# Attention and mixture-of-experts kernel on one core: the additions of the output and the second conditionings at other units, and a new order around the last unit

## What is computed

```python
ek = exp(min(f, 30)); ekv = ek * f
a, b = scan forward and backward over tokens: a = a*decay + ekv, b = b*decay + ek
out = sigmoid(r) * (num / max(den, 1e-8)) * (0.8 + 0.2*tf)        # r is x or the later x
x = x + attention(cond(x, f, f))      # 16 heads of 128, causal mask, softmax, output weights W_O
x = x + ffn(cond2(x, f, f))           # 8 experts; top 2 by the logits, softmax of the two as gates
```

## Time and profile before

| | before |
|---|---|
| median of three runs | 371.82 us |
| the profiled execution, its own time | 371.82 us |
| its span (first to last instruction) | 369.9 us |
| busy: TensorE matmul, VectorE, ScalarE, GpSimd | 93%, 86%, 69%, 57% |
| mean granted TensorE clock | 0.995 |

### The profile page before, as it was taken

The page is one execution under the profiler, slowest core; times in us unless marked ns, Lnnn a source line. Parts: engine busy times, 40 slices in busy tenths (PEclk is TensorE's granted clock), DMA queues, the critical chain, the costliest instruction groups (busy, mean ns, idle before and its releaser), DMA issues.

```text
span 369.9 us, 7426 instructions
## 1 busy us (share of the span) xinstructions
PE 344.7 (93%) x2404; PEld 319.4 (86%) x2404; DVE 318.7 (86%) x892; ACT 255.9 (69%) x687; POOL 212.6 (57%) x223
## 2 busy tenths in 40 slices
PE   0796599999999999999999999999999989899997
PEld 0685499998999999989999999999999979788885
DVE  4979899999898989899989999999768576869675
ACT  5669888788878869886888888878778565321100
POOL 1875686855756468867867886787673424210000
PEclk9999989999999999999999999999999999999999
DMA  5670130100000000130100022100000000000000
GB/s 166 240 276 4 57 113 2 59 4 1 2 0 3 1 2 0 52 123 0 28 31 3 1 73 101 58 3 1 2 2 1 2 1 2 0 16 15 28 28 30
DMA packets 4613, 14.13 MB, mean 38 GB/s; under 512 B 848, under 2 KB 1888, under 8 KB 3936
## 3 DMA queue, kind: packets, MB, share of 16 engines
q1 hardware_dynamic: 4352, 13.66, 11.0%
q10 hardware_dynamic: 224, 0.01, 0.0%
HBM read 12.60 MB, written 1.05 MB: 37 GB/s over the span
## 4 chain that ended last, share of the span: by engine, by line
PE 63%; DVE 28%; ACT 3%; issue 3%; DMA 1%; DVEq 0%; ACTq 0%
PE psQK L947 7%; PE psQK L949 7%; PE psQK L948 7%; DVE tiles L729 4%; PE psT L1017 4%; PE psO L947 3%; PE psS L947 3%; PE psS L949 3%; PE psS L948 3%; PE psO L949 3%; PE psO L948 3%; PE psV L947 3%; PE psS L1003 3%; PE psZ L1030 3%; PE psV L948 3%
## 5 line engine op out<-in xcount | busy, mean ns | idle before, releaser
L324 POOL TENSOR_SCALAR prob<-prob,rsum 128x256 f32<-128x256 f32 x60 | 55.5, 925 | 63.1 <-DVE rsum L764 63.1
L947 PE MATMUL psQK<-y_hi,w_hi 128*128 128x256 f32 x256 | 72.2, 282 | 1.1 <-DVE y_lo L679 1.1
L518 ACT ACTIVATE prob<-prob,ntop 128x256 f32<-128x256 f32 (+1 forms) x128 | 57.0, 448 | 23.1 <-DVE ntop L756 23.0
L949 PE MATMUL psQK<-y_hi,w_lo 128*128 128x256 f32 x256 | 72.3, 282 | 0.0
L948 PE MATMUL psQK<-y_lo,w_hi 128*128 128x256 f32 x256 | 72.2, 282 | 0.0
L330 POOL TENSOR_TENSOR z_lo<-z_lo,z_two 128x256 fp32r<-128x256 f32 x64 | 48.2, 753 | 33.7 <-DVE z_lo L782 33.7
L289 POOL TENSOR_TENSOR w_lo<-raw,w_hi 128x512 fp32r<-128x512 f32 x40 | 53.7, 1352 | 11.2 <-ACT w_hi L383 11.1
L947 PEld LDWEIGHTS psQK<-y_hi,w_hi 128*128 128x128 f32 x256 | 48.6, 190 | 2.9 <-issue 1.5
L948 PEld LDWEIGHTS psQK<-y_lo,w_hi 128*128 128x128 f32 x256 | 48.6, 190 | 1.3
L949 PEld LDWEIGHTS psQK<-y_hi,w_lo 128*128 128x128 f32 x256 | 48.7, 190 | 0.0
L506 ACT ACTIVATE qk<-psQK 128x512 fp32r<-128x512 f32 x64 | 37.6, 587 | 15.1 <-PE psQK L949 14.8
(11 more groups left out here) (166 smaller groups left out, 1039.1 us busy)
## 6 DMA issues: line engine op xcount, KB each, us to landing
raw<-in_weights SPq DMA_DIRECT2D x5, 1024.0 KB, 5.3
raw<-in_weights SPq DMA_DIRECT2D x10, 512.0 KB, 4.2
out<-fT SPq DMA_DIRECT2D x8, 128.0 KB, 1.7
fT<-in_fT SPq DMA_DIRECT2D x2, 256.0 KB, 5.0
xT<-in_xT SPq DMA_DIRECT2D x2, 256.0 KB, 6.8
fT<-in_fT SPq DMA_DIRECT2D x1, 512.0 KB, 6.2
xT<-in_xT SPq DMA_DIRECT2D x1, 512.0 KB, 6.2
temb<-in_temb ACTq DMA_DIRECT2D x1, 1.0 KB, 3.3
```

Of the source, the lines that this page charges most:

```text
L324: pool.tensor_scalar(prob[:, k, P:3 * P], prob[:, k, P:3 * P], rsum[:, k, 1:2], None, ALU.mult).then_inc(shared, 1)
L518: ins = act.activation(prob[:, k, lo:hi], prob[:, k, lo:hi], ACT.Exp, scale=-1.0, bias=ntop[:, k, q:q + 1], accum_out=ssum[:, k, q:q + 1])
L947: pe.matmul(out, ah, bh, start=first and k == 0, stop=False)
L949: ins = pe.matmul(out, al, bh, start=False, stop=last and k == n - 1)
```

## The change

The second conditionings (numbers 4 to 7) start two units later, so each of their pieces moves by two units on VectorE, ScalarE and GpSimd. The addition of a block's output to x (`add_output`, L785) moves for blocks 0 to 11 from place M of a V unit (h = 1) to place E of the next one (h = 2). The transposes of the first batch's gates move from unit 61 to unit 63, its `base` from ahead of the transposes of unit 62 to behind `values` of unit 61, with the copies and sums that follow. On VectorE, behind the last unit, the low part of z of unit 62 moves ahead of the second batch's gates (`gate_last(1)`). The weight refills stay where they were.

```diff
--- before.py
+++ after.py
@@ -49,7 +49,7 @@
 
 
 CONDS = [(b, w) for w in (0, 1) for b in range(B)]
-COND_START = (None, None, 5, 13, 21, 29, 37, 45)
+COND_START = (None, None, 5, 13, 23, 31, 39, 47)
 COND_DVE, COND_ACT, COND_POOL = (13, 13), (9, 7), (5, 5)
 DVE_PLACES = {"min": (-3, "E"), "xd": (0, "M"), "xn": (1, "M"), "gd": (2, "M"), "gn": (3, "M"), "den": (4, "M"),
               "r0": (5, "M"), "r1": (6, "M"), "y": (7, "M")}
@@ -557,10 +557,9 @@
         at(57, "E", tanh, 0)
         at(58, "E", y2_high, 0)
         at(60, "E", gate_exp, 0)
-        at(61, "E", gates_copy, 0)
+        at(63, "M", gates_copy, 0)
         at(61, "E", tanh, 1)
         at(62, "E", y2_high, 1)
-        at(63, "E", base_copy, 0)
 
         def do(u, place):
             for f, args in work.get((u, place), ()):
@@ -596,6 +595,7 @@
             do(u, "E")
         pT_high(UNITS - 2)
         z_high(UNITS - 3)
+        base_copy(0)
         gate_exp(1)
         pT_high(UNITS - 1)
         tanh(2)
@@ -863,13 +863,16 @@
         at(10, "M", late_rests)
         at(12, "M", bias_low_part)
         for i in range(len(BLOCKS) - 2):
-            at(GH * (i + 2) + 1, "M", add_output, i)
+
+            if i < 12:
+                at(GH * (i + 2) + 2, "E", add_output, i)
+            else:
+                at(GH * (i + 2) + 1, "M", add_output, i)
         at(58, "M", y2_last, 0)
         at(60, "M", gate_first, 0)
         at(61, "M", gate_last, 0)
-        at(62, "M", gT_low, 0)
+        at(63, "M", gT_low, 0)
         at(62, "M", y2_last, 1)
-        at(63, "E", add_experts, 0)
 
         def do(u, place):
             for f, args in work.get((u, place), ()):
@@ -909,12 +912,13 @@
         pT_low(UNITS - 2)
         z_low(UNITS - 3)
         gate_first(1)
+        add_experts(0)
         add_experts(1)
         add_output(14)
+        pT_low(UNITS - 1)
+        z_low(UNITS - 2)
+        gate_last(1)
         add_experts(2)
-        pT_low(UNITS - 1)
-        gate_last(1)
-        z_low(UNITS - 2)
         y2_last(2)
         add_experts(3)
         z_low(UNITS - 1)
@@ -987,8 +991,6 @@
             pe.wait_ge(wlo_v, 2 * (g + 1))
             y_waits(b)
             pe.wait_ge(v_ready, TT * i + t)
-            if TT * i + t == TT * len(BLOCKS) - 1:
-                pe.wait_ge(gT_ready, 1)
             for c in range(CB):
                 ins = project_v_half(i, t, c)
             ins.then_inc(v_done, 1)
@@ -1060,7 +1062,7 @@
             if b:
                 pe.wait_ge(base_added, b)
             else:
-                pe.wait_ge(v_ready, TT * len(BLOCKS) - 1)
+                pe.wait_ge(v_ready, TT * len(BLOCKS))
             for t in range(TT):
                 ins = pe.transpose(psG[:, t * P:(t + 1) * P], gates_two[:, b, t].rearrange("p a e -> p (a e)"), identf[:])
             ins.then_inc(gT_done, 1)
@@ -1068,8 +1070,6 @@
         def base(b):
             if b:
                 pe.wait_ge(base_added, b)
-            else:
-                pe.wait_ge(v_ready, TT * len(BLOCKS))
             pe.wait_ge(x_added, 13 + b)
             pe.wait_ge(gT_ready, b + 1)
             if b == 0:
@@ -1137,6 +1137,8 @@
             scores(u)
             if u == UNITS - 2:
                 experts(0)
+            if u == UNITS - 1:
+                gates_turn(0)
 
             if 1 <= h <= TT and i > 0:
                 project_v(i, h - 1)
@@ -1150,15 +1152,12 @@
                 output(i - 1, 0)
             if h == 0 and i >= 2:
                 output(i - 2, 1)
-            if u == UNITS - 1:
-                base(0)
             if u:
                 turn(u - 1)
-            if u == UNITS - 3:
-                gates_turn(0)
             if u >= UNITS - 2:
                 if u == UNITS - 1:
                     values(UNITS - 3)
+                    base(0)
                 experts(u - UNITS + 3)
         output(len(BLOCKS) - 2, 1)
         turn(UNITS - 1)
```

## The result

| | before | changed |
|---|---|---|
| median | 371.83 us (11 runs, 371.73 to 372.01 and one of 373.25) | 373.69 us (11 runs, 373.54 to 373.91) |
| span of the profiled execution | 369.9 us | 371.9 us |
| busy: TensorE, VectorE, ScalarE, GpSimd | 93%, 86%, 69%, 57% | 93%, 86%, 69%, 58% |

The ratio is 1.005, with a 95% interval of 1.0042 to 1.0057: slower by 1.9 us, where 374.0 was forecast. The score starts on TensorE's timeline (line 1003 is now 1005) answer to the earlier trace rows: units 24, 26, 27, 28, 30, 31, 32.

The account below looks back on a forecast made before the run. TensorE was taken as the bound (93% busy), so its waits count: -2.9 stalls, +5.8 turns, +0.5 GpSimd's load, +0.4 exponentials, -1.6 end gave +2.2 on 371.82, so 374.0 us, range 368.0 to 375.8.

Parts of the forecast that it names:

- turns beside gn: Units 26, 34, 41, 42, 49, 50: gn's or gd's scans alternate with GpSimd's instructions, making VectorE late; +5.8 us.
- A: The main forecast: around 374.0 us (372.9 to 375.5), slower than before, chance 0.47.
- rival C: Refills of units 41 and 49 come too late to be met; the h = 2 places lose +4.0, 372.2 us, chance 0.15.
- exponentials on ScalarE: At h = 1, beside a refill at the end of 29, 37, 45, they make the next pT_low late; +0.4 us.
- end: Around the last unit three waits worth 3.1 us go, but z_low(63) behind gate_last(1) holds the last projection; 1.6 kept.
- limit S + 4.43: In h = 2, M must end within 4.43 us of the unit's start S, or TensorE waits as long.
- B: Rival: gn's second scan gets in ahead of the refill, no turns in V units; 368.2 us, chance 0.28.
- its clamp is over at about S + 2.3: Units 41 and 49: GpSimd is early, its refill asks during the first scan; 0.5 us lost, twice.
- At place E of h = 2 the addition costs 0, up to 0.2 if VectorE doesn't catch up: The moved output addition stands behind z_low and delays only the next unit's maxima, where VectorE catches up.
- at unit 13 that alone brings M to 1.9, the limit, so the 0.6 lost at 14 goes: Taking the output addition (0.6 us) out of M in unit 13 removes unit 14's stall.
- Now it holds one reciprocal, below 1.92, all four stalls go: M at 29, 37, 45 loses its scan pair and addition; stalls at 14, 30, 38, 46 vanish, -2.9 us.
- 319.52 - 317.72 = 1.80: Length in us of gate_last(1) on VectorE before z_low(63), taken from the earlier trace.

Follow-up runs that it names:

- refills off gn: The changed kernel with the four weight refills beside gn (GpSimd's units 26, 34, 42, 50) one unit later, those behind as needed: 371.03 us, ratio 0.9981.
- refills off y: The changed kernel with the two refills beside y (GpSimd's units 38 and 46) one unit later: 374.04 us, ratio 1.0059.
- conditionings only: The kernel before with only the second conditionings' start units moved to 23, 31, 39, 47: 377.44 us, ratio 1.0156.
- The last experiment: Changed kernel, second conditionings back, z_low(63) behind experts step 2, and of the moved additions only those of odd blocks kept: 367.86 us, ratio 0.9893.
- best so far: The changed kernel with the second conditionings back where they were and z_low(63) right behind experts step 2: 369.33 us, ratio 0.9933.
- z low early: The changed kernel with z_low(63) on VectorE right behind experts step 2 instead of behind the third y and step 3: 372.62 us, ratio 1.0021.

## Why the prediction was right, and where it was not

Forecast 374.0, measured 373.69. The direction and the main cost, turns beside gn at h = 2, were A's. At units 41 and 49 it was rival C that came true (turns at h = 2 only, chance 0.15, 372.2). That the total lies within 0.3 of A's number is luck: every term was off, two losses put too high (by 2.4 and 0.3) against two gains put too high and one loss put too low (by 1.4, 0.55 and 0.6). The differences of the table's columns, by the prediction's own terms:

| term | predicted | measured |
|---|---|---|
| stalls behind the first scans (14; 30 and 31; 38; 46) | -2.9 | -0.14 - 0.50 - 0.50 - 0.38 = -1.5 |
| turns beside gn (27, 35, 43, 51) and what V loses | +5.8 | 3 x 0.86 + 0.83 = +3.4 |
| GpSimd's load (28, 29) | +0.5 | +0.2 |
| exponentials on ScalarE (39, 47) | +0.4 | +0.5 + 0.5 = +1.0 |
| end | -1.6 | -1.05 |
| sum | +2.2 | +2.0 |

The start of the profile, before unit 8, is 0.13 shorter, no more than it differs among the other kernels, which makes +1.9, as the medians have it.

- *Turns at h = 2.* Right, down to the pair's length (2.8 to 3.2 predicted, 3.03 to 3.05) and the limit S + 4.43 (units 27 and 39 lose some 0.1 more than VectorE was past it); B is refuted by the trace and by "refills off gn". The Trainium skill (page SBUF — State Buffer, section "SBUF: two separate sides") has whichever engine starts first hold the shared ports for its whole instruction. The pair of 3.05 beside 1.29 and 1.67 agrees. The pair of unit 41, which started during the clamp (209.58 against 208.68 to 210.17) and took 1.26, does not.
- *Units 41 and 49.* Here C was right: the refill came too late to be met. The step that failed is "its clamp is over at about S + 2.3"; it was over at S + 2.76 (210.17 - 207.41), later by the stall at 39, of which the prediction had put 0.1. In the kernels without that stall it is over at S + 2.44 to 2.55, and the refill is met. No V wait followed, and so 42 and 50 were on time, and 43 and 51 lost 0.83 and 0.86 instead of 1.4 each. Two other kernels, "refills off y" and "conditionings only", show what the step had described, 0.4 to 1.0 and then 1.2. Of the 5.8 predicted, 2.4 was not there: 1.0 at 42 and 50, 1.1 at 43 and 51, 0.3 at 27 and 35.
- *"At place E of h = 2 the addition costs 0, up to 0.2 if VectorE doesn't catch up".* This step failed at unit 14, and with it "at unit 13 that alone brings M to 1.9, the limit, so the 0.6 lost at 14 goes". M started at S + 2.56 (84.77 - 82.21), not at S + 2.18. The last experiment shows why: lateness is carried over for units.
- *"Now it holds one reciprocal, below 1.92, all four stalls go".* True at 38 and 46. Unit 30 kept 0.63: VectorE began unit 29 at S + 2.02 (155.02 - 153.00), behind a reciprocal and the minimum in unit 28. The minimum had moved too, and I had not priced it. It takes 0.42 alone (144.73 in "best so far") and took 1.20 beside refills:

```profile
153.90 1.20 DVE L697 TENSOR_SCALAR tiles<-fT 128x512 f32<-128x512 f32 x1
```

- *Exponentials.* Mis-sized: 0.1 each at 39 and 47, measured 0.5 (the 0.1 each at 38 and 46 was not there). The refill in the same place, y's turn behind it, and no slack in h = 2 make it; "refills off y" shows all of it going. This miss and the one at 41 and 49 belong together: with the stall gone, "refills off y" has 1.4 of the 2.4 back.
- *End.* The mechanism (z_low(63) behind gate_last(1)) was right, the size was 1.05 for 1.6. On the old clock (2.88 less, the difference of the starts of unit 61, 297.40 - 294.52) z_low(62) came at 316.4 for 316.3, so its place was right. The step that failed is "319.52 - 317.72 = 1.80" for the gates: with z_low(62) ahead of them, z_last(62) runs beside them, and they took 2.17. z_low(63) came at 321.36 for 320.9 and the projection at 322.68 for 322.2.

The additions' move is worth 0.35 by itself and, if the end gives its 0.97 there too, 377.44 - 0.97 - 373.69 = 2.8 beside the moved conditionings. In M at h = 1 the addition stands behind gd's pair: with a pair of 2.31 units 42 and 50 lose 0.98 and 0.97 there, and 0.40 and 0.38 in "refills off y", where it stands elsewhere. The pair of edits without the end was not run.

## What to carry to other kernels

Where two engines take turns, list for every unit when each asks, with the lateness that the units before hand on, and treat an order decided by a few hundredths of a microsecond as either. A filler instruction should go where the units behind it have slack, not merely to a unit that has some. Take out a stall and look again: it may have been holding a later pair apart.

## What the runs showed of the hardware beyond what was expected

- Two instructions that wait for the same GpSimd instruction to end, one on each engine, were served in either order in two executions whose recorded starts differ by 0.01: 1.36 or 2.62 for the same y in the same place.
- VectorE's minimum, with one input, waits for GpSimd's refills too (0.42 alone, 1.20 beside them). A GpSimd clamp with one input let a pair of scans pass in 1.26, as if it were not there; the earlier trace rows had 1.51 beside one.
- A small instruction waits as well: the gates' product of 128x2 takes 0.51 or 0.52 beside z_last in all ten kernels with the new end, and 0.16 in the kernel before (at 318.11), with GpSimd idle.
- GpSimd waits as well: z_last took 1.12 beside the third y in "z low early" where it takes 0.73.

```profile
323.22 1.12 POOL L330 TENSOR_TENSOR z_lo<-z_lo,z_two 128x256 fp32r<-128x256 f32 x1 [2.69 <-DVE z_lo L782]
```
